# Cross attention of the third layer: the output projection as three one-pass products of split operands

## What is computed

```
kv_c = kv @ W_kvc                      # (.., 64) latents
q_c  = q @ W_dq                        # (.., 96)
q_nope = (q_c @ W_uq) per head (128);  q_rope = rope(q_c @ W_qr) per head (64)
k_nope = kv_c @ W_uk;  v = kv_c @ W_uv;  k_rope = rope(kv_c @ W_kr)
scores = (q_nope . k_nope + q_rope . k_rope) * scale, masked by seg_id
out = softmax(scores) @ v, heads side by side;   return out @ W_o
```

## Time and profile before

| what | value |
|---|---|
| median of 3 runs | 2408.22 us (2404.01 to 2409.35) |
| profiled execution | 2404.21 us, its span 2402.4 us |
| granted TensorE clock, mean | 0.937 of 2.4 GHz |
| TensorE (products) busy | 2116.3 us, 88% |
| TensorE (weight loads) busy | 1600.0 us, 67% |
| VectorE busy | 1585.9 us, 66% |
| ScalarE busy | 1237.8 us, 52% |
| GpSimd busy | 294.7 us, 12% |
| output products L3068 | 62.3 us busy in 256 records of 128x256, for 128 products |

### The profile page before, as it was taken

How to read it: one execution, slowest core, us unless ns; L and a number is a source line. 1 busy time by engine, 2 the same in 40 slices (tenths; PEclk the granted TensorE clock), 3 DMA queues, 4 the chain that set the end, 5 groups by cost and what they waited for, 6 DMA issues and landing times. The chain is left out here.

```text
span 2402.4 us, 46894 instructions
## 1 busy us (share of the span) xinstructions
PE 2116.3 (88%) x18960; PEld 1600.0 (67%) x18963; DVE 1585.9 (66%) x2975; ACT 1237.8 (52%) x2457; POOL 294.7 (12%) x301
## 2 busy tenths in 40 slices
PE   7979979899899898888889998957989879999996
PEld 5644437677655687566656666646656667999996
DVE  4433476666565897877848666787666676676663
ACT  3336714444466443655536446644467724566653
POOL 0010000010210000001000000000100111444342
PEclk9989989899999998999999999978989978999998
DMA  2020001100110002000010010010200024766673
GB/s 98 21 81 10 2 20 48 36 1 1 40 37 2 33 1 70 1 1 1 1 32 1 9 61 0 0 35 1 71 1 2 6 71 169 220 202 199 203 220 86
DMA packets 62649, 125.59 MB, mean 52 GB/s; under 512 B 16056, under 2 KB 45369, under 8 KB 62297
## 3 DMA queue, kind: packets, MB, share of 16 engines
q1 hardware_dynamic: 53626, 110.83, 13.5%
q0 software_dynamic: 8832, 12.06, 2.4%
HBM read 109.18 MB, written 15.80 MB: 52 GB/s over the span
## 5 line engine op out<-in xcount | busy, mean ns | idle before, releaser
L262 PE MATMUL ps<-ffn_xh,ffn_wh 128*128 128x256 f32 x644 | 184.0, 286 | 1.5 <-DVE ffn_xl L4228 1.5
L262 PE MATMUL ps<-ffn_xh,ffn_wl 128*128 128x256 f32 x644 | 182.2, 283 | 0.0
L262 PE MATMUL ps<-ffn_xl,ffn_wh 128*128 128x256 f32 x644 | 182.1, 283 | 0.0
L4223 DVE TENSOR_TENSOR ffn_wl<-ffn_fresh,ffn_wh 128x1792 fp32r<-128x1792 f32 x69 | 139.3, 2022 | 26.3 <-ACT ffn_wh L4101 26.2
L1886 DVE SCALAR_TENSOR_TENSOR attn_xc<-attn_cx,all_w,attn_xc 128x512 f32<-128x512 f32 (+1 forms) x144 | 107.3, 749 | 50.3 <-ACT attn_xc L1737 46.7
L210 POOL TENSOR_TENSOR all_rstd<-all_mv,all_cst 128x4 f32<-128x4 f32 x41 | 9.6, 233 | 1066.8 <-DVE all_mv L193 1066.7
L262 PEld LDWEIGHTS ps<-ffn_xh,ffn_wh 128*128 128x128 f32 x644 | 123.3, 192 | 1.7 <-DVE ffn_xl L4228 1.7
L4101 ACT ACTIVATE ffn_wh<-ffn_fresh 128x1792 fp32r<-128x1792 f32 x69 | 116.9, 1694 | 13.6 <-DMA ffn_fresh<-in_l3f_w 13.6
L262 PEld LDWEIGHTS ps<-ffn_xl,ffn_wh 128*128 128x128 f32 x644 | 123.4, 192 | 0.0
L262 PEld LDWEIGHTS ps<-ffn_xh,ffn_wl 128*128 128x128 f32 x644 | 123.3, 192 | 0.0
L2880 ACT ACTIVATE xattn_sc<-xattn_sc,xattn_mx 128x128 f32<-128x128 f32 x256 | 98.8, 391 | 17.7 <-DVE xattn_mx L2955 17.7
(11 more groups left out here) (484 smaller groups left out, 6100.6 us busy)
## 6 DMA issues: line engine op xcount, KB each, us to landing
ffn_fresh<-in_l3f_w SPq DMA_DIRECT2D x69, 896.0 KB, 4.7
all_w<-in_ctxT SPq DMA_DIRECT2D x12, 512.0 KB, 6.1
all_w<-in_ctx SPq DMA_DIRECT2D x8, 512.0 KB, 6.3
all_x<-in_x_rows SPq DMA_DIRECT2D x4, 512.0 KB, 7.4
all_x<-x_seq SPq DMA_DIRECT2D x4, 512.0 KB, 5.3
all_w<-in_l2x_o SPq DMA_DIRECT2D x1, 2048.0 KB, 9.1
xattn_ctxT<-in_ctxT SPq DMA_DIRECT2D x4, 512.0 KB, 3.9
all_w<-in_l2f_up SPq DMA_DIRECT2D x1, 2048.0 KB, 9.1
```

The lines of the kernel that those rows point to most:

```text
L262: last = pe.matmul(out, a, b, start=start and n == 0, stop=stop and n == 2)
L4223: dve.tensor_tensor(wl[:, j % 2, piece(q)], fresh[:, piece(q)], wh[:, j % 2, piece(q)].bitcast(F32), ALU.subtract).then_inc(low_ready.sem, 1)
```

## The change

The output weights and the weighted latents are split into a rounded part and a rest. In the preparation ScalarE writes `woh` in place of `wvo` and VectorE subtracts `wol`, so that the bank is free after the subtraction. In the loop `copy_out` writes `zh` in place of `zT`, and VectorE has a new function `low`, called for unit n-2 in iterations 2 to 9 between `find_max(n)` and `normalize(n-1)`. TensorE's `project_out` makes three one-pass products for each full one; it and the next `weigh` wait for the rest in place of the copy.

```diff
-    wvo = k.sb("wvo", [P, PAIRS, D])
+    woh = k.sb("wo_high", [P, PAIRS, D], F32R)
+    wol = k.sb("wo_low", [P, PAIRS, D], F32R)
...
-    zT = k.sb("zT", [P, 2, 4, P])
+    zh = k.sb("z_high", [P, 2, 4, P], F32R)
+    zl = k.sb("z_low", [P, 2, 4, P], F32R)
...
-                    if 2 <= n < 6:
+                    if n >= 2:
                         pe.wait_ge(*split(0, n - 1))
-                    if n >= 6:
-                        pe.wait_ge(*copied(0, n - 5))
...
-                        act.activation(wvo[:, n - 4, :], k.psum[n % 2][:, 0:D], ACT.Copy).then_inc(copied.sem, 1)
+                        act.activation(woh[:, n - 4, :], k.psum[n % 2][:, 0:D], ACT.Copy).then_inc(high_set.sem, 1)
...
+                for n in range(4, N):
+                    dve.wait_ge(*high_set(0, n + 1))
+                    dve.tensor_tensor(wol[:, n - 4, :], k.psum[n % 2][:, 0:D], woh[:, n - 4, :].bitcast(F32),
                                       ALU.subtract).then_inc(split.sem, 1)
...
-                    act.activation(zT[:, n % 2], Z[:, :].rearrange("p (j l) -> p j l", j=4), ACT.Copy).then_inc(zT_ready.sem, 1)
+                    act.activation(zh[:, n % 2], Z[:, :].rearrange("p (j l) -> p j l", j=4), ACT.Copy).then_inc(zh_ready.sem, 1)
...
+                def low(n):
+                    dve.wait_ge(*zh_ready(i, n + 1))
+                    dve.tensor_tensor(zl[:, n % 2], Z[:, :].rearrange("p (j l) -> p j l", j=4), zh[:, n % 2].bitcast(F32),
+                                      ALU.subtract).then_inc(zl_ready.sem, 1)
...
                         find_max(n, 0)
                         find_max(n, 1)
+                    if 2 <= n <= U + 1:
+                        low(n - 2)
                     if 1 <= n <= U:
                         normalize(n - 1)
...
                     if n >= 1:
-                        pe.wait_ge(*zT_ready(i, n))
+                        pe.wait_ge(*zl_ready(i, n))
...
-                    pe.wait_ge(*zT_ready(i, n + 1))
+                    pe.wait_ge(*zl_ready(i, n + 1))
...
-                        last = pe.matmul(O[:, 0:D], zT[:, n % 2, j, :], wvo[:, 4 * w + j, :], start=w == 0 and j == 0,
-                                         stop=w == W - 1 and j == 3)
+                        last = three(pe, O[:, 0:D], (zh, zl), (woh, wol), (slice(None), n % 2, j, slice(None)),
+                                     (slice(None), 4 * w + j, slice(None)), w == 0 and j == 0, w == W - 1 and j == 3)
```

More of the change, by code:

```diff
@@ L2754, in phase_xattn2 @@
         split = Signal(k, "products_split")
-        copied = Signal(k, "products_copied")
         high_set = Signal(k, "high_set")
@@ L2810, in _ @@
                                       wh[:, LAT, 2 * n:2 * n + 2, :].rearrange("p a b -> p (a b)").bitcast(F32),
+                                      ALU.subtract).then_inc(split.sem, 1)
+                for n in range(4, N):
+                    dve.wait_ge(*high_set(0, n + 1))
+                    dve.tensor_tensor(wol[:, n - 4, :], k.psum[n % 2][:, 0:D], woh[:, n - 4, :].bitcast(F32),
                                       ALU.subtract).then_inc(split.sem, 1)
@@ L2843, in phase_xattn2 @@
     z_psum = Signal(k, "z_psum", U)
-    zT_ready = Signal(k, "zT_ready", U)
+    zh_ready = Signal(k, "z_high_ready", U)
+    zl_ready = Signal(k, "z_low_ready", U)
     out_psum = Signal(k, "out_psum", TG)
```

## The result

| kernel | median | runs | ratio to before, 95% interval |
|---|---|---|---|
| before | 2408.78 us | 4 (2404.01 to 2410.68) | |
| changed | 2486.02 us | 4 (2483.52 to 2494.67) | 1.0331 [1.0308, 1.0354] |

The change costs 77 us, 3.3%. The profiled execution is the longest of the four (2494.67 us, span 2492.9), 8.7 us above the median. From the first product of the preparation to the last add the stage takes 419.0 us (1234.6 to 1653.6) where it took 339.0 (1228.7 to 1567.7). The other 10.5 us of the span's difference lie in other stages, whose code is the same: 6.0 ahead of the stage and 4.6 behind it.

A forecast was written before the change was run, and what follows sets the result against it. It took TensorE as closest to the bound on average, but a closed 7.62 us chain as the new floor. Groups 67.7, preparation 1.5 and clock 3 sum to 72.2; on 2404.2, plus 4 for the median, 2480 us, range 2464 to 2502.

The forecast's parts named there:

- The wait closes a loop of 7.62 us: Unit loop: the subtraction waits behind ScalarE's exponentials, so one closed chain of 7.62 us is an iteration's lower bound.
- The additions: Norm and add work on VectorE in some iterations, atop 7.62: 1.73 us in n=3, 0.43 in n=5 and n=7, 1.37 in n=5.
- The rival that ScalarE's own way, over transposes and copies, ends later: Unit loop: exp(n+1) behind copy_probs(n-1) is later than VectorE's way by 0.5 us; +10, 2490 us; 7 in 100.
- The subtraction's duration: VectorE's low(n) in the loop: nearest row 0.687 us, 0.61 from start to start.
- One-pass products save 0.39 us a unit: TensorE's output products: twelve at 0.120 us, 1.44 for 1.83; a gain only where TensorE sets the time.
- The group's end, +1.9 us: From exp(7) to the last add: +2.7 up to weigh(7), then two projections 0.39 shorter each; 1.9 a group.
- Preparation, +1.5 us: Output-weight copies: VectorE subtracts before a bank is free, 0.86 us each, plus 0.4 for later copies; bounds 0 and +4.
- Clock, 3 us, between 0 and 6: Iteration 2: TensorE idles 3.4 us, scores(5) may run at half speed, 1.5 a group; 3 taken.
- The rival of a clock that stays low all through: Whole loop: TensorE falls to 1.2 GHz and stays there, 71 us more, 2551 us; 4 in 100.
- The waiting of VectorE: Before the subtraction, for ScalarE's copy: about 3 us in each of n=2 to 7, 70 to 90 us in all.

The follow-up runs named there:

- e1: Kernel before with only the subtraction added in the changed kernel's place, its result unused, weigh and project_out waiting for it; 2489.75 us, 1.0342.
- e3: Changed kernel with each subtraction one iteration later, low(n-3) in place of low(n-2), nothing left out; 2403.9 us, 0.9986 of the kernel before.
- e4: Changed kernel with unread filler products in TensorE's gaps in the loop, iterations 2 to 8; 2478.13 us, 1.0302 of the kernel before.
- e5: Changed kernel with low(n-2) called after normalize(n-1) instead of before it, same iteration; 2439.61 us, 1.0136 of the kernel before.
- e6: e3 with the next norm's statistics moved after find_max(3) and its normalizing from n=5 to n=7; 2399.28 us, 0.9967 of the kernel before.
- e2: Changed kernel without the subtraction in the loop, z_low set to zero once, the twelve one-pass products kept; 2400.15 us, 0.9962 of the kernel before.

## Why the prediction was right

It forecast 2480 us for a measured 2486.02, by the mechanism that the runs show. Its steps:

- **The wait closes a loop of 7.62 us.** Shown by e1 (the wait alone brings the slowdown), e3 (one iteration later removes it), e4 (7.66 us with the clock held) and e5 (1.43 us out of the chain, 1.43 off the period). The additions held as well: 9.35 us forecast and measured from unit 2 to 3, 8.05 for 7.99, 8.99 for 8.95. The rival that ScalarE's own way, over transposes and copies, ends later did not come: the first exponentials of units 3 to 6 waited 0.48 to 1.77 us for VectorE's maxima in the first group. As the Trainium skill says of ScalarE and VectorE (TensorE: Matmul & The Clock Gate, "Architectural detail: the array is 16× 32×32, not 1× 128×128"), both kept their strict order; e3 and e5 differ from the changed kernel by that order alone.
- **The subtraction's duration**, 0.69 us and 0.61 from start to start, was 0.69 (128x512) and 0.60 (1300.01 to 1300.61).
- **One-pass products save 0.39 us a unit.** Mis-sized a little: 0.34. In a row of twelve the first start to the second takes 0.22 us and the others 0.11 to 0.12. The formula of the Trainium skill (TensorE: Matmul & The Clock Gate, "Back-to-back issue gap"), N / 2.4 + 2.5 for an isolated product and so 109 ns, would have given a saving of 0.52 as an estimate and is further off.
- **The group's end, +1.9 us.** Mis-sized: 2.6, 2.5 and 3.2 us between groups (47.74, 47.63 and 48.37 less 45.16) and 3.2 at the last. From exp(7) to weigh(7) the first group took 12.77 us (1339.84 to 1352.61), forecast 12.2; the transposes and copies cost more signals than I had put in. In the last two groups the clock was low once more while unit 6 was weighed (1.82 and 1.87 us where 1.08 is usual), which makes their ends 3.2. Four ends: 11.5 us for 7.6.
- **Preparation, +1.5 us.** About right. The copies' pace was forecast as 0.86 us and is 0.89, as the rows below this list show. From the first product to the first exponential the profiled execution took 54.6 us against 51.7, so +2.9. But e3, e4, e5 and e6 have the same preparation and took 52.9, so +1.2. The rest belongs to this one execution: the idle products that follow took 8.41 us at a granted clock of 0.64, where the kernel before took 7.08 at 0.76 and e3 some 6.8 at 0.79.
- **Clock, 3 us, between 0 and 6.** Mis-sized: it came to the upper bound and a little over. The clock fell in every group. Units 3 to 4 are 0.9, 1.2, 1.7 and 1.65 us over 7.62, and in the first group 5 to 6 is 0.7 over: 6.2 us, and some 1.3 more are in the ends of the last two groups. The gap of 3.4 us was there, 3.33. e4 gives 7.9 us for what it took away. The rival of a clock that stays low all through did not come, but the short gaps did not keep it either. In each group it fell again in iteration 5 or 6, with gaps of only 0.5 to 1.6 us ahead of it, and stayed low for 3 to 13 us; there it hardly delayed the chain, since TensorE had time to spare. The Trainium skill (TensorE: Matmul & The Clock Gate, "HAM oscillation — how this bites in real kernels") describes a kernel whose TensorE comes out of each long wait between two bursts of products at the lower clock. The long gap of each group agrees with it, 0.50 after 3.33 us; the falls behind short gaps are not what that section describes.

The preparation of the changed kernel (rows 7 answer to these):

```profile
L2796 ACT ACTIVATE xattn_wo_high<-ps x8: 383/384/384, 1240.4 to 1246.6; 128x256 fp32r<-128x256 f32 x8
L2813 DVE TENSOR_TENSOR xattn_wo_low<-ps,xattn_wo_high x8: 424/425/425, 1240.8 to 1247.0; 128x256 fp32r<-128x256 f32 x8
```

In the profiled execution the parts add up to the stage's 80 us: 65.7 between units 2 and 7 of four groups (forecast 60.1 without the clock), 11.5 at the ends, 2.9 ahead. The forecast is 6 us under the measured median: the ends were put 4 us and the clock at least 3 us too low, and no term was off the other way by more than 1, so the hit owes nothing to errors that cancel. The waiting of VectorE was forecast at 70 to 90 us and was 109.7; the forecast had left out the subtractions of n = 8 and 9.

The 4.6 us behind the stage are within what executions scatter: from the last add to the end of the program the profiled executions of all twelve kernels take 830 to 839 us (834.7 before, 839.3 changed, 833.9 for e4, whose loop has the same chain). What stays open is why the clock fell behind the short gaps.

## What to carry to other kernels

Before a subtraction or copy is put into a hand-written order, ask not only whether its engine has time, but how far that engine runs ahead of the one it will wait for. Here VectorE was one unit ahead of ScalarE, and an operation of 0.6 us that waited at that point cost 2 to 4 us a round; the same operation one iteration later cost 3.8 us in all 32 times (e3 against e2). Add up the chain through all queues back to the same operation: if the sum is larger than today's period, it is a floor for the new one, whatever the busy shares say. Here 7.62 us against 5.79, and the period came to 7.66 where the clock was held.

## What the runs showed of the hardware

- After 3.33 us of idle time within an otherwise busy loop TensorE worked at 1.2 GHz (granted clock 0.50 from 1303 to 1306) and was at 2.4 GHz again by 1309, after some 3 us of scores.
- Gaps of 0.5 to 1.6 us can also be followed by 1.2 GHz: in the second group, after gaps of 1.21, 0.54, 1.54 and 0.69 us, the granted clock was 0.50 from 1429 to 1441. The kernel before, whose gaps in the loop are fewer, had 1.00 in the same iterations.
- Useless products in TensorE's gaps (5.2 us of them in iteration 2 of each group, 0.9 in each of the next six) made the whole kernel 7.9 us faster.
- Eight transposes whose second half waits for VectorE's second multiplication take 1.26 us, 1.04 when both are ready.
